# Up and gate weights of the second layer: half sums on GpSimd ahead of the Hadamard matmul

## What is computed

```
x = input.reshape(-1, n)                         # n = 256
x = fwht(x * SU_ug) / SCALE
x_up = x @ W_up.T * (Wscale_ug[:INTER] * SCALE)  # INTER = 1024
x_gate = x @ W_gate.T * (Wscale_ug[INTER:] * SCALE)
x = silu(x_gate) * x_up
x = fwht(x * SU_dp) / SCALE
x = x @ W_down.T * (Wscale_dp * SCALE)
```

## Time and profile before

| | before |
|---|---|
| median of 3 runs | 781.52 us (779.87 to 783.82) |
| profiled execution, its own time | 779.61 us |
| its span in the trace | 777.8 us |
| TensorE busy | 712.5 us, 92% |
| VectorE busy | 550.7 us, 71% |
| ScalarE busy | 435.9 us, 56% |
| GpSimd busy | 288.7 us, 37% |
| chain that ended last | TensorE 73%, VectorE 13%, ScalarE 5%, GpSimd 3% |
| mean granted TensorE clock | 0.969 |

### The profile page before, as it was taken

The page is one execution under the profiler, slowest core; times in us unless marked ns, Lnnn a source line. Parts: engine busy times, 40 slices in busy tenths (PEclk is TensorE's granted clock), DMA queues, the critical chain, the costliest instruction groups (busy, mean ns, idle before and its releaser), DMA issues.

```text
span 777.8 us, 10975 instructions
## 1 busy us (share of the span) xinstructions
PE 712.5 (92%) x4190; PEld 446.3 (57%) x4190; DVE 550.7 (71%) x896; ACT 435.9 (56%) x579; POOL 288.7 (37%) x273
## 2 busy tenths in 40 slices
PE   3778898969697979999999999999999999999997
PEld 3657787957456868867767676333333433333444
DVE  4897766675557674667888878888888378888416
ACT  2542223345244444243243333999999899999883
POOL 0156865332314566343344343012224213422510
PEclk9898999998799989999999999999999999999999
DMA  6145101000301345334311002344344345342221
GB/s 247 55 155 186 52 0 55 1 1 1 108 0 40 125 155 196 103 106 146 110 55 55 24 32 72 108 131 132 113 138 140 90 133 172 126 131 84 95 85 55
DMA packets 25704, 74.14 MB, mean 95 GB/s; under 512 B 4604, under 2 KB 5980, under 8 KB 24692
## 3 DMA queue, kind: packets, MB, share of 16 engines
q1 hardware_dynamic: 21124, 65.37, 25.1%
q0 software_dynamic: 3808, 7.60, 3.3%
q10 hardware_dynamic: 720, 0.48, 0.2%
HBM read 54.54 MB, written 23.06 MB: 100 GB/s over the span
## 4 chain that ended last, share of the span: by engine, by line
PE 73%; DVE 13%; ACT 5%; issue 4%; POOL 3%; DMA 1%; SPq 0%; DVEq 0%; ACTq 0%; POOLq 0%
PE PS L734 23%; PE PS L996 16%; PE PS L982 11%; PE PS L740 10%; PE PS L965 6%; PE PS L955 4%; DMA stg<-in_wa 1%; DVE mx L1275 1%; DVE XD L1081 1%; PE PS L814 1%; DVE sg L1213 1%; DVE sg L1204 1%; DVE XL L1088 1%; ACT sg L1415 1%; DVE bst L1066 1%
## 5 line engine op out<-in xcount | busy, mean ns | idle before, releaser
L1461 ACT ACTIVATE P<-PS 128x1024 f32<-128x1024 f32 x256 | 249.0, 1024 | 29.9 <-PE PS L982 29.7
L1282 DVE TENSOR_REDUCE mx<-PS 128x1 f32<-128x512 f32 x300 | 189.1, 682 | 32.1 <-PE PS L965 30.5
L1275 DVE TENSOR_REDUCE mx<-PS 128x2 f32<-128x1024 f32 x106 | 124.8, 1220 | 37.9 <-PE PS L955 37.6
L996 PE MATMUL PS<-P,VV 128*32 128x512 f32 x1024 | 136.5, 605 | 0.1
L1538 POOL TENSOR_TENSOR hl<-sg,hh 128x512 fp32r<-128x512 f32 x64 | 83.1, 1299 | 137.1 <-ACT hh L1423 79.9
L982 PEld LDWEIGHTS PS<-QS,KS 64*128 64x128 f32 x512 | 48.4, 183 | 123.2 <-ACT P L1461 110.2
L982 PE MATMUL PS<-QS,KS 64*128 64x512 f32 x512 | 116.6, 456 | 2.3 <-DVE mx L1275 1.8
L965 PE MATMUL PS<-KM,QM 64*128 64x512 f32 x300 | 81.3, 396 | 0.0
L1417 ACT ACTIVATE sg<-PS,cols 128x512 f32<-128x512 f32 x32 | 22.0, 688 | 83.0 <-PE PS L734 83.0
L734 PE MATMUL PS<-XH,UGH 128*128 128x512 f32 x128 | 54.9, 429 | 5.8 <-ACT us L1426 4.9
L1547 POOL TENSOR_TENSOR sg<-sg,us 128x512 f32<-128x512 f32 x32 | 42.1, 1315 | 37.2 <-ACT us L1426 37.2
(11 more groups left out here) (201 smaller groups left out, 1417.5 us busy)
## 6 DMA issues: line engine op xcount, KB each, us to landing
QM<-scr_q SPq DMA_DIRECT2D x16, 512.0 KB, 4.3
KM<-scr_k SPq DMA_DIRECT2D x16, 512.0 KB, 5.3
QS<-scr_q SPq DMA_DIRECT2D x16, 512.0 KB, 4.3
KS<-scr_k SPq DMA_DIRECT2D x16, 512.0 KB, 5.3
scr_q<-spl SPq DMA_DIRECT2D x24, 256.0 KB, 3.3
scr_k<-spl SPq DMA_DIRECT2D x24, 256.0 KB, 3.6
scr_o<-OE POOLq DMA_DIRECT2D x14, 256.0 KB, 2.7
stg<-in_tern SPq DMA_DIRECT2D x3, 1024.0 KB, 4.8
```

The lines of the kernel that those rows point to most:

```text
L996: i = e.matmul(PS[32 * c:32 * c + 32, 7, :], v_head(8 * b + kt, 2 * j + c // 2), P[s % 4][:, chunk(c // 2 + 2 * (c % 2))], start=(kt == 0) ...
L1275: e.tensor_reduce(mx[p % 2][:, :, qt, half], PS[:, b:b + 2, :], AX.X, ALU.max).then_inc(q["mx"], 2)
L1282: e.tensor_reduce(mx[p % 2][:, h, qt, half:half + 1], bank[b], AX.X, ALU.max).then_inc(q["mx"], 1)
L1461: e.activation(P[s % 4][:, half * 1024:(half + 1) * 1024], PS[:, b:b + 2, :].rearrange("p b n -> p (b n)"), ACT.Exp).then_inc(q["ex"], 1)
```

## The change

GpSimd gets a new piece, `halves_ug(n)`, n = 0 for up and 1 for gate. It writes `lo - hi` to a new tile `DIF[n]` and then, in place, `lo + hi` over `lo` in the staging tile; the second operation follows the first by the count `hs`. `prep_ug` then needs one matmul per step, `HAD` with the sum or with the difference, and waits on `hs` in the first step of each kind. `DIF[0]` is at 198 (the place of `XD[2]`), `DIF[1]` at 190 (the place of `stg2`), which adds two waits: `halves_ug(1)` on the fourth `prep_down` matmul, and `ln_norm` 6 on the first four `prep_ug` matmuls. `HADN` goes; the wait for the constants' loads in `signs` moves to VectorE's first `kv_in`, and the one for the scaled signs of the down matrix to ScalarE's first `prep_down`. The two pieces stand in the list behind `prep_down` 1 and before `prep_ug` 0. The functions of TensorE, GpSimd and the list:

```diff
@@ work_order, side0
         for q in range(4):
             put("prep_down", q, ps.next())
             yield
+            if q == 1:
+                put("halves_ug", 0)
+        put("halves_ug", 1)
         for u in range(8):
             put("prep_ug", u, ps.next())
             yield
@@ program
-        HADN = sb("HADN", 25, [128, 128])
+        DIF = [sb(f"DIF{i}", (198, 190)[i], [128, 1024]) for i in range(2)]
@@ TensorE
             def prep_ug(u, b):
                 n, k, h = u // 4, u // 2 % 2, u % 2
-                i, value = STAGE["up" if n == 0 else "gate"]
-                raw = stg[i][:, :].rearrange("p (k n) -> p k n", k=2)
-                hs = slice(h * 512, (h + 1) * 512)
+                src = DIF[n] if k else stg[n][:, 0:1024]
                 claim(b)
-                e.wait_ge(d[f"st{i}"], value)
-                e.wait_ge(q["sus"], 3)
-                sums(bank[b], [(HAD[:, :], raw[:, 0, hs]), ((HADN if k else HAD)[:, :], raw[:, 1, hs])]).then_inc(q["pu"], 1)
+                if h == 0:
+                    e.wait_ge(q["hs"], 2 * n + 2)
+                e.matmul(bank[b], HAD[:, :], src[:, h * 512:(h + 1) * 512], start=True, stop=True).then_inc(q["pu"], 1)
                 freed[b] = q["ul"], u + 1
@@ VectorE, ln_norm
+                if n == 6:
+                    e.wait_ge(q["pu"], 4)
@@ VectorE, signs
-                e.wait_ge(d["c"], 64)
-                e.tensor_scalar(HADN[:, :], HAD[:, :], -1.0, None, ALU.mult).then_inc(q["sus"], 1)
@@ VectorE, kv_in
+                if tt == 0:
+                    e.wait_ge(d["c"], 64)
@@ ScalarE, prep_down
+                if n == 0:
+                    e.wait_ge(q["sus"], 2)
@@ GpSimd
+            def halves_ug(n):
+
+                i, value = STAGE["up" if n == 0 else "gate"]
+                lo, hi = stg[i][:, 0:1024], stg[i][:, 1024:2048]
+                e.wait_ge(d[f"st{i}"], value)
+                if n == 1:
+                    e.wait_ge(q["pd"], 4)
+                e.tensor_tensor(DIF[n][:, :], lo, hi, ALU.subtract).then_inc(q["hs"], 1)
+                e.wait_ge(q["hs"], 2 * n + 1)
+                e.tensor_tensor(lo, lo, hi, ALU.add).then_inc(q["hs"], 1)
```

More of the change, by code:

```diff
@@ L35 @@
 g u t v1 ue h hh hl d
-w1h w1l vbb vbm ob bf pd dh dl pu uh ul
+w1h w1l vbb vbm ob bf pd dh dl hs pu uh ul
 qk rs rg sh sl vp vv vones
@@ L1608, in low @@
                     e.wait_ge(q["fill"], 2)
-            parts = {f.__name__: f for f in (bias, fold, kv_in, q0, butterfly, prep_attn1, up, hidden, ones_v, qk, load_wl, out, recip, times, high, low)}
+            parts = {f.__name__: f for f in (bias, fold, kv_in, q0, butterfly, prep_attn1, halves_ug, up, hidden, ones_v, qk, load_wl, out, recip, times, high, low)}
             for name, *args in order:
```

## The result

The changed kernel takes **775.76 us** in the median of five runs (773.14 to 777.41), against 781.52 us (779.87 to 783.82) for the kernel before, run beside it. The ratio is **0.9934, with a 95% interval of 0.9913 to 0.9955**: by the ratio 5.2 us, or 0.7%, faster. The profiled execution took 775.39 us (span 773.6, mean granted clock 0.960); that of before took 779.61 us (span 777.8, clock 0.969).

A forecast was written before the change was run, and what follows sets the result against it. TensorE bounds the kernel, busy 712.5 of 777.8 us. Saving 6.9 us, less 1.6 us of waits and 0.2 us of VectorE's queue, leaves 5.1: 781.52 - 5.1 = 776.4 us, range 773.5 to 780.4.

The forecast's parts named there:

- The price of a matmul: TensorE, up and gate preparation: one matmul takes 0.86 us, so the eight removed save 6.9 us.
- The waits and the negation at nothing: Moved waits end nothing; dropping VectorE's HADN negation at 23.04 us saves 0 to 0.22 us, taken as 0.
- GpSimd's cover: Four added GpSimd operations of 2.4 us stay hidden: 1.8 us of cover before ug0, 6 us before ug4.
- What becomes late next: Banks given back by VectorE's UGL: TensorE waits before ug7 and qk, 1.6 us; VectorE's queue costs another 0.2 us.
- The sum of the stretch: Up to the first `rot`: 6.9 us less 1.6 and 0.2 leaves 5.1 us, `rot` at 229.7 instead of 234.8.
- Every later stage as long as before.: After `rot`: the matmul of 248.89 starts at 243.8 and every later stage keeps its length.
- (a): Rival, preparation's PSUM banks: they don't bind, all of 6.9 to 7.7 us comes through, 773.8 to 774.6; chance 0.16.
- (b): Rival, TensorE's clock falls in the new gaps, costing 1.7 to 4 us: 778.1 to 780.4; chance 0.14.
- (c): Rival, a fixed point in the chain between 237 and 249 us absorbs the gain: 779.5 to 781.5; chance 0.11.
- (d): Rival, GpSimd's new operations run much longer; loses from 5.5 us each, over 785.4 from 6.4; chance 0.05 with clock variant.
- a mutual slowing of VectorE and GpSimd: During GpSimd's new operations: the rows show none, and it would cost nothing up to the ug1 matmul.

The follow-up runs named there:

- half of the change: Changed kernel with sums on GpSimd for the up matrix only, the gate matrix keeping two matmuls and HADN: 777.64 us, ratio 0.996.
- The three-bank run: Changed kernel with the eight preparation matmuls going round three PSUM banks in place of two: 774.98 us, ratio 0.9923.
- the first run with both later: Changed kernel with GpSimd's low parts, ScalarE's copies of the attention weights and the gate's load moved behind prep_down 1: 772.03 us, ratio 0.9885.

## Why the prediction was right, step by step

**The price of a matmul** (0.86 us, eight of them 6.9). Right: half of the change gave 3.43 of 3.44 us, with 0.1 us between single traces, and issuing each twice took back all of it.

**The waits and the negation at nothing.** Right, by the same run: 31.97 us with all of the additions and none of the gain, 31.98 before.

**GpSimd's cover.** Right. Operations of 2.35 to 2.39 us (2.4), the first pair done at 206.6 (207.3), ug0 at 208.32 with no wait (209.05), 1.7 us of cover (1.8). The second pair waited 0.38 us for the fourth down matmul, as the forecast order had it, and no one waited for the pair. One reading there was wrong, without a cost: of VectorE's operations beside the new ones I wrote that TensorE waits for none, but it waits 0.56 us for XL ahead of the fourth down matmul, before the change as after it. XL, which reads a PSUM bank, takes 0.69 us beside GpSimd's new operations as without them, so they don't slow it.

**What becomes late next.** Right in kind. Both waits are where they were laid out, before ug7 and before qk, ended by UGL: 0.47 and 0.56 us of idleness, 0.63 and 0.72 counted as the forecast did, from start to start, where it had 0.7 and 0.8 (and 1.6 for their sum, which is 1.5). The tiles came at distances of 3.88 and 3.21 us (4.0 and 3.2 forecast). `rot` started behind VectorE's own queue and not behind TensorE. But the sum read these waits as a price of the banks, "1.6 us of it comes back as two waits". The three-bank run shows that they are no price by themselves: with the bank free, the same time stands in one wait, since the two engines behind set the pace.

**The sum of the stretch**, 5.1 us forecast, 5.66 measured. The mis-sized term is the start of the last chunk. I had its first hh at 218.6, which is 15.8 us after the transposes; it came 15.39 us after them. The first distance between tiles was 0.12 us shorter than laid out, and the way from the third hh to `rot` 0.06. Most of the 0.4 us belongs to this execution and not to the change: the clock rose 7.7 us after the transposes (0.52 in the microsecond from 209, 1.00 from 210), where it had risen 8.4 us after them before. In the change's second trace it rose 7.9 us after them, and the first hh came at 15.49; with three banks and with the up matrix alone it rose after 8.3 and 8.5 us, and the first hh came at 15.68 and 15.73, nearly the forecast's 15.8.

**"Every later stage as long as before."** True from `rot` up to the softmax stage, which began 6.2 us ahead, of which 0.58 stood there before the change's place; false in this one execution for the stage itself, by 2 us of low clock. The forecast named as its own refutation "if the 5 us seen at 235 are smaller at 300": they weren't (6.2 us at 242.67), and smaller only at 480. The kernel before pays it too in some executions. The ratio gives 5.2 us, with 3.5 to 6.8 by its interval (the two medians differ by 5.8), so it can't tell whether a part of the 5.66 us is lost there on average. That it lies within 0.1 us of the forecast's 5.1 is in part luck: in the two traces, 5.66 us were gained in the stretch, 0.58 ahead of it, and 1.9 lost behind it.

**The rivals.** (a) that everything comes through holds for the first half only, as the up-matrix run shows. (b) the clock in the new gaps: it was 1.00 throughout from 223 to 235, so waits of 0.47 and 0.56 us didn't lower it; with a wait of 3.08 us ahead of ug0, where it was at 0.50 already, it was still there six us behind the wait, which cost some 2 us beside the wait itself. That is a rise that came later and not a fall, so no run shows the rival's mechanism in this stretch; behind the change, the waits of 1.18 and 0.63 us were followed by a fall, but in the kernel before they were too. (c) nothing fixed behind absorbed the gain: the changed kernel's lead is 6.2 us at 242.67, 6.1 at 275.30 and 6.2 at the first P. (d) GpSimd's operations: with twice as many of them (9.6 us in place of 4.8 ahead of ug0) the kernel ended level with the one before, while I had written that twice the duration would still save some 2.7 us. The clock was left out there: the stretch was 31.71 us long, so 0.3 us was saved in place of 2.7.

**A row that I had and didn't read.** I wrote that the rows show nothing of a mutual slowing of VectorE and GpSimd. The trace of before has it, at 194.66, where the normalization takes 3.79 us. It changed nothing in the forecast, since the change doesn't touch that place, but the 2.4 us between 3.79 and 1.38 are nearly half of what the change gained.

## What to carry to other kernels

Time taken from the busiest engine arrives whole up to the point where the next engine's queue sets the pace; lay that engine's instructions out in their order, with the distances between starts of the old trace, and see when its queue is free, rather than counting the waits of the faster engine. Start the engine that will carry the chain as early as may be: work put ahead of its first instruction costs in full, even where it spares the last one. Before an addition goes to GpSimd or to VectorE, look at what the other one does at that time between SBUF and SBUF, and which of the two is being waited for: here the slower engine was the better place, because nobody waited for it. And read a gain from more than one trace of each kernel, stage by stage, where the clock changes from one execution to the next.

## What the runs showed of the hardware

**VectorE and GpSimd take turns.** The normalization is four VectorE operations, SBUF to SBUF. Alone one takes 0.40 to 0.41 us (the four 1.38 together, since recorded durations overlap, in the run with GpSimd's low parts moved away). In the change, VectorE's first two, from the timeline cut into single instructions:

```profile
194.09 0.89 DVE L1084 TENSOR_SCALAR XD<-X,mv,rstd 128x256 f32<-128x256 f32 x1
```

```profile
194.90 1.38 DVE L1084 TENSOR_SCALAR XD<-X,mv,rstd 128x256 f32<-128x256 f32 x1
```

and GpSimd's beside them:

```profile
191.37 3.46 POOL L1550 TENSOR_TENSOR W1L<-stg,W1H 128x1536 fp32r<-128x1536 f32 x1 [3.69 <-ACT W1H L1394]
194.78 1.34 POOL L1550 TENSOR_TENSOR WOL<-stg,WOH 128x512 fp32r<-128x512 f32 x1
196.08 1.30 POOL L1554 TENSOR_TENSOR hl<-sg,hh 128x512 fp32r<-128x512 f32 x1
```

GpSimd's three end at 194.83, 196.12 and 197.38; VectorE's end at 194.98, 196.28 and, the third, at 197.54, each 0.15 to 0.16 us behind one of them. The fourth, beside which GpSimd did nothing, took 0.40 us. That isn't a shared rate: an operation that takes 0.4 us waits out a whole GpSimd operation. VectorE's operations on a PSUM bank are untouched: the DL pair takes 0.88 us at 193.09 beside W1L, and 0.88 us at 205.36 in the first run with both later, where GpSimd is idle. The Trainium skill, "SBUF — State Buffer", section "SBUF: two separate sides", states it: the read and write ports that the two share are locked for a whole instruction, by whichever starts first, against VectorE operations in a two-port mode or with two SBUF inputs, these only against a GpSimd operation that reads SBUF. The traces agree, with 3.78 us against 1.38, and with the additions on VectorE (two SBUF inputs) of 1.61 and 2.17 us against 1.22. The normalization has one SBUF input beside its per-row scalars; no trace shows whether it ran in a two-port mode.

**The clock is no function of the waits alone.** The same two waits, 1.18 and 0.63 us, were followed by 1.00 in one execution and by 0.50 in the other, and the mean clocks of twelve executions of the kernel before spread from 0.958 to 0.974. A difference of 2 us between two single traces of this kernel says nothing about a change; two kernels' traces must be compared stage by stage.
